# Delta rule: the affine step of the transposed output written back into its PSUM bank, the gate product reading it there

## What is computed

```python
def step(S, inp):
    qt, kt, vt, at, bt = inp
    err = jnp.einsum('bhvk,bhk->bhv', S, kt) - vt
    S = at[..., None, None] * S - bt[..., None, None] * err[..., None] * kt[:, :, None, :]
    o = jnp.einsum('bhvk,bhk->bhv', S, qt)
    return (S, o)
...
mu = o.mean(-1, keepdims=True)
var = ((o - mu) ** 2).mean(-1, keepdims=True)
o = (o - mu) * jax.lax.rsqrt(var + 1e-05) * ln_w + ln_b
g = jax.nn.sigmoid(x @ Wg).reshape(B, T, H, DV)
o = (o * g).reshape(B, T, H * DV)
return o @ Wo
```

## Time and profile before

| what | value |
|---|---|
| time, 3 runs | 2032.39, 2032.53 and 2035.86 us, median 2032.53 us |
| the profiled execution | span 2036.0 us, from its first to its last instruction; no other time of it is given |
| delta rule in steady work | stages of 39.3 to 39.6 us, two in turn 78.9 us; X steps from 752 us to 1954 us |
| busy over the span | PE 94%, DVE 80%, ACT 64%, POOL 35% |

### The profile page before, as it was taken

One profiled execution on the slowest core, in us unless ns is written; L12 is line 12 of the kernel. 1 busy time (PEld: TensorE's weight loads), 2 busy tenths in 40 slices (PEclk: granted clock), 3 DMA queues, 4 the chain that ended last, 5 costly groups with the idle time before them and its releaser, 6 DMA issues.

```text
span 2036.0 us, 64584 instructions
## 1 busy us (share of the span) xinstructions
PE 1912.4 (94%) x27132; PEld 1441.0 (71%) x27132; DVE 1636.3 (80%) x3073; ACT 1296.8 (64%) x2818; POOL 722.7 (35%) x993
## 2 busy tenths in 40 slices
PE   8699999998985899999999999999999999999877
PEld 4233333326874688888888888888888888888766
DVE  6799989954654688888888888888888888888566
ACT  3088888894423466666667666666766666676563
POOL 1244445443231233343333423432433433333233
PEclk9599999999986899999999999999999999999989
DMA  5211221201001111101111111111111011010101
GB/s 175 74 27 38 53 55 32 58 8 27 1 1 51 44 33 36 36 24 47 38 31 47 33 37 39 41 36 37 44 36 37 30 50 36 23 36 26 46 1 42
DMA packets 74191, 79.57 MB, mean 39 GB/s; under 512 B 13296, under 2 KB 60784, under 8 KB 73904
## 3 DMA queue, kind: packets, MB, share of 16 engines
q1 hardware_dynamic: 73904, 75.44, 12.6%
HBM read 66.11 MB, written 8.91 MB: 37 GB/s over the span
## 4 chain that ended last, share of the span: by engine, by line
PE 55%; DVE 7%; ACT 3%; POOL 2%; issue 2%; POOLq 0%; DVEq 0%; ACTq 0%
PE ps L1505 15%; PE ps L1533 5%; PE ps L1554 4%; PE ps L1577 4%; PE ps L1617 3%; PE ps L1641 3%; PE ps L1635 2%; PE ps L1665 2%; PE ps L1624 2%; POOL d_above L1457 2%; ACT d_ad L1717 2%; PE ps L1647 2%; DVE d_o_g L1880 2%; PE ps L1606 2%; PE ps L1612 2%
## 5 line engine op out<-in xcount | busy, mean ns | idle before, releaser
L1806 DVE SCALAR_TENSOR_TENSOR d_acc<-ps,d_par,d_acc 128x1023 f32<-128x1023 f32 (+2 forms) x288 | 363.6, 1263 | 16.6 <-ACT d_acc L1688 14.7
L1505 PE MATMUL ps<-x1p,d_wh 128*128 128x512 f32 x1024 | 358.7, 432 | 14.4 <-DVE d_acc L1806 9.6
L592 ACT ACTIVATE a_prob<-ps 128x512 f32<-128x512 f32 (+2 forms) x640 | 309.2, 562 | 91.7 <-PE ps L558 86.3
L614 DVE TENSOR_REDUCE a_mx<-ps 128x2 f32<-128x1024 f32 (+2 forms) x320 | 335.0, 1110 | 27.9 <-PE ps L542 21.9
L1688 ACT ACTIVATE d_acc<-ps,d_par 128x512 f32<-128x512 f32 x192 | 148.9, 776 | 143.3 <-PE ps L1505 138.7
L1440 POOL TENSOR_TENSOR d_og_l<-d_o_g,d_og_h 128x512 fp32r<-128x512 f32 x64 | 82.4, 1289 | 353.9 <-ACT d_og_h L1784 353.9
L1505 PE MATMUL ps<-x1p,d_wl 128*128 128x512 f32 x512 | 205.0, 400 | 0.0
L1505 PEld LDWEIGHTS ps<-x1p,d_wh 128*128 128x128 f32 x1024 | 173.2, 194 | 38.4 <-DVE d_acc L1806 10.8
L537 PE MATMUL ps<-k,q 48*128 48x512 bf16 (+3 forms) x768 | 155.9, 351 | 25.1 <-DVE a_mx L614 14.8
L558 PE MATMUL ps<-q,k 51*128 51x512 bf16 (+2 forms) x640 | 175.8, 365 | 1.8 <-ACT a_prob L592 0.9
L503 POOL TENSOR_SCALAR_AFFINE_SELECT a_prob<-a_prob 128x128 f32<-128x128 f32 (+1 forms) x384 | 125.9, 332 | 124.7 <-ACT a_prob L592 114.0
(11 more groups left out here) (245 smaller groups left out, 4762.7 us busy)
## 6 DMA issues: line engine op xcount, KB each, us to landing
d_abc<-scratch_alpha SPq DMA_DIRECT2D x32, 512.0 KB, 4.1
d_gb<-scratch_g SPq DMA_DIRECT2D x32, 512.0 KB, 3.9
d_wr<-in_dw SPq DMA_DIRECT2D x16, 512.0 KB, 5.1
scratch_q<-p_parts SPq DMA_DIRECT2D x24, 128.0 KB, 2.4
q<-scratch_q SPq DMA_DIRECT2D x32, 96.0 KB
scratch_y<-a_oT SPq DMA_DIRECT2D x64, 36.0 KB
x_tok<-in_x SPq DMA_DIRECT2D x4, 512.0 KB, 7.2
q<-scratch_q SPq DMA_DIRECT2D x32, 64.0 KB
```

The costliest lines, as they stand in the source:

```text
L592: inc(nc.scalar.activation(prob[:, y % PB, g:g + heads, off:], ps[:, PLACE["st", n, x], 0:heads * w].rearrange("p (h c) -> p h c", c=w), A ...
L614: inc(nc.vector.tensor_reduce(out, ps[:, bank:bank + 2, 0:heads * w].rearrange("p r (h c) -> p r h c", c=w), AX.X, ALU.max, negate=True), ...
L1505: last = nc.tensor.matmul(ps[:, bank, :], wp[g][:, k, i, :], x(part), start=(k == 0 and j == 0), stop=(k == KE - 1 and j == 2))
L1806: inc(nc.vector.scalar_tensor_tensor(acc[i][:, d:T], taps[:, 0:T - d], par[p][:, 4 * i + j:4 * i + j + 1], acc[i][:, d:T], ALU.mult, ALU.a ...
```

## The change

ACT's affine step writes its result into the PSUM bank that it reads, and not into `o_g`. The DVE's gate product reads that bank and `gate`, and writes `o_g`. The guard that `o_g`'s buffer is free again (`og_l` of unit n-2) moves from ACT to the DVE. And since the bank is now in use up to the gate product, the ring names `gated` as the reader of an o_turn, and not `affine`.

```diff
@@ PE
         def o_turn(n, j):
-            bank = ring(n, ("o_turn", j), ("affine", n, j + 1))
+            bank = ring(n, ("o_turn", j), ("gated", n, j + 1))
             W("normed", n, j + 1)
@@ ACT
             W("o_turned", n, j + 1)
-            W("og_l", n - 2, j + 1)
-            inc(nc.scalar.activation(o_g[n % 2][:, j * HALF:(j + 1) * HALF], ps[:, BANK[n, "o_turn", j], :], ACT.Identity, bias=ln2[:, 1:2],
-                                     scale=ln2[:, 0:1]), "affine")
+            bank = ps[:, BANK[n, "o_turn", j], :]
+            inc(nc.scalar.activation(bank, bank, ACT.Identity, bias=ln2[:, 1:2], scale=ln2[:, 0:1]), "affine")
@@ DVE
         def o_turn(n, j):
             W("affine", n, j + 1)
+            W("og_l", n - 2, j + 1)
             c = slice(j * HALF, (j + 1) * HALF)
-            inc(nc.vector.scalar_tensor_tensor(o_g[n % 2][:, c], gate[n % 2][:, c], 1.0, o_g[n % 2][:, c], ALU.add, ALU.mult), "gated")
+            inc(nc.vector.scalar_tensor_tensor(o_g[n % 2][:, c], gate[n % 2][:, c], 1.0, ps[:, BANK[n, "o_turn", j], :], ALU.add, ALU.mult), "gated")
```

## The result

The changed kernel is slower: 2045.75 us in the median of 5 runs (2042.83 to 2049.02) against 2033.8 us before (5 runs, 2032.39 to 2038.85). The ratio is 1.0054, with a 95% interval of 1.0038 to 1.0069, so 8 to 14 us. Forecast were 2050.0 us and 17.5 us more.

The account below looks back on a forecast made before the run. PE was taken as the bound, busy 1064.16 of 1070 us. Stall +20.7 and gain -3.2 make +17.5 on the profile's 2036.0 us, so 2053.5; carrying over its 3.5 us above the runs' median gives 2050.0 us, range 2041 to 2057.

Parts of the forecast that it names:

- the stall: At X.o_turn.1 (L1653), PE's loads wait for the end of half 0's gate product: 0.69 us in 30 stages, 20.7 us.
- the gain: Faster product shortens PE's wait at L1617: 0.21 us in 14 stages, 2.9 us, plus 0.3 us in stage 34; 3.2 us.
- The 0.1 us that I allowed: At PE's restart after each stop: possibly 0.1 us more to get going, 3 us on top over 30 stages.
- no later wait takes it up: Behind the stalled transposes: no later PE wait shrinks, so 0.69 us stays in each stage; rival of large take-up, chance 0.08.
- The product: The DVE's gate product L1880, with one operand in PSUM: 0.67 us instead of 1.69, 65 us less DVE busy time.
- that second wait: PE's loads waiting for the state (L1863), 4.4 us in 15 stages: the only place where a saved DVE microsecond counts.
- The hidden places: S.v_turn.1 hidden by 3 us, the L1834 wait gains nothing, ACT's PSUM write hidden: taken as no cost.
- that rival: PE's clock falls where it stands still: 1 us in each of 30 stages, 2080 us; chance 0.07 together with slower PSUM steps.
- Two stages in turn: Length of two successive stages in the changed kernel's profile: 80.0 to 80.1 us, not 78.9.

Follow-up runs that it names:

- e5_twice: The changed kernel with one more gate product of half 0, into a scratch tile, directly ahead of the real one: 2061.81 us, ratio 1.0126.
- e1_ring_only: The kernel before, with only the reader that the ring waits for changed from affine step to gate product: 2068.5 us, ratio 1.0168.
- e2_relief_only: The kernel before and its ring, gate product replaced by a DVE transpose of one SBUF operand (doesn't compute the reference): 2025.95 us, ratio 0.9960.
- e3: The changed kernel with PE's X.o_turn.1 moved behind S.oc.1.0 and S.oc.1.1: 2027.22 us, ratio 0.9965.
- e4: The changed kernel with the DVE's product of half 0 moved ahead of step qd.1.1 (units 0 to 29): 2028.32 us, ratio 0.9971.
- e7: The kernel before, with PE's X.o_turn.1 behind S.oc.1.0 and S.oc.1.1 and the ring waiting for the gate product: 2042.84 us, ratio 1.0035.
- e9_qg_last: The kernel before, with GpSimd's step qg (L1446) moved behind X.og.1: 2025.3 us, ratio 0.9960.
- e8_order_half: The kernel before, with PE's X.o_turn.1 moved only behind S.oc.1.0: 2043.29 us, ratio 1.0043.
- e6_order_only: The kernel before, with only PE's X.o_turn.1 moved behind S.oc.1.0 and S.oc.1.1: 2029.23 us, ratio 0.9965.

## Why the prediction was right, and where it was off

The direction and the mechanism of the loss were right, and the time lies in the range; the net was too large, 17.5 us against 12. Both terms were off to the same side, the stall somewhat too large and the gain too small.

- **The stall.** Forecast 0.69 us a stage in 30 stages, 20.7 us. The loads start 0.67 us later against the product, but PE's first matmul now starts with its load and not 0.11 us behind it, and the piece from L1577 to L1624 is 0.62 us longer, 18.6 us in 30 stages. The 0.1 us that I allowed for a slower start after a stall isn't there.
- **That no later wait takes it up.** Right for the sum, and for any further delay: e5_twice moves the product's end by 0.60 us and the stage by 0.58. But e1_ring_only shows that the stall does take up the waits at L1617 and w.7, without relief. In the changed kernel both would have gone either way, and each can go only once, so the sum of stall and gain holds.
- **The product.** Forecast 0.67 us, measured 0.665 on average (42.6 us in 64), also beside POOL. The DVE's group fell by 65.7 us, forecast 65.
- **The gain.** This is the step that was off: "The gain is 3.2 us". It measures 7.1 us in the 29 stages alone (e2_relief_only). At L1617 it is 3.4 us, where I had 2.9; at w.7 it is 2.6, where I had nothing. I had taken it from the one wait in the list that the slow product stands ahead of, and the list has no waits this short: the load at L1635 followed its releaser by 0.05 us in every stage, and that is the mark of a wait, but I read only rows with a time in brackets. The difference of 4 us is most of the error. It also makes the sentence wrong that a microsecond of the DVE is worth something only at that second wait.
- **The hidden places.** S.v_turn.1 doesn't wait, the wait for L1834 stays at 9.0 us, PE's clock stays at 1.00 from 780 to 1850 us, and ACT's step in PSUM is hidden (0.75 us for 0.78). All as forecast. That the clock can fall after a longer stop shows in e1_ring_only: 1.6 us for each time, against the 1 us put down for that rival.
- **Two stages in turn**: forecast 80.0 to 80.1, measured 79.73.

Of the two parts, the wait is shown by e1 (it comes with the ring), e3, e4 and e7 (it goes when PE comes later, the DVE earlier, or the product ends sooner) and e5 (its slope). That relief at L1617 and w.7 comes from the end of the contention of the half 1 product is shown by e9_qg_last, which gets it with the product and the ring left as they were. What stays open is some 1 us of the 7.1 in e2_relief_only, spread over short steps.

## What to carry to other kernels

A buffer that is handed on in place lives until its last reader; ask which engine reuses it next and how long after the new reader's start it arrives. Here TensorE wanted the bank of a two-deep ring again 0.03 us after the new reader's start. That cost it 0.62 us in each of 30 stages, more than 65 us less of VectorE's time gave. Where the bound engine reaches the new wait a little too early, something else of its queue can go ahead of it (e3_pe_late), and where a slow operation is slow because of a neighbour, moving the neighbour is the smaller change (e9_qg_last). And when looking for what an engine waits for, look also at loads that start within 0.05 us of their releaser's end, stage after stage: they carry no idle time in the list and add up all the same.

## What the runs showed of the hardware

- Between GpSimd's L1446 or L782 and the gate product with two SBUF operands, the first to start is the one that is served. With POOL 0.50 us ahead the product takes 2.43 us and POOL its 2.37 (e8_order_half); with POOL 0.06 us behind, the product takes 0.68 us and POOL 2.86 (e6_order_only). The held product ends 0.55 us behind POOL; the held POOL takes 0.49 us more. With one of the product's operands in PSUM, neither is held: 0.65 to 0.69 us, and 2.37 for POOL's L1446, which is running when the product starts (changed kernel).
- ScalarE's affine step on 128x512 takes 0.748 us in the median when it writes into PSUM (min 0.722, max 0.752), and 0.776 us into SBUF (0.762 to 0.793). It is hidden here.
- Four transposes of full tiles between two steps of 32x32 tiles cost PE 0.24 us more than ahead of both: the piece from L1577 to L1624 takes 2.74 us in e8_order_half, 2.51 before, and 2.46 with the transposes behind both (e6_order_only).
- After a stop of 1.73 us, TensorE's granted clock fell to 1.2 GHz for 3.4 us in 2 of 14 stages of e1_ring_only, and each of these two stages took 1.6 us more.
